# Sliding-window attention and a gated feed-forward on eight cores: earlier slots, a bias that comes by transfer, and mixing on two engines

## The reference

```python
q, k, v = x @ Wq + bq, x @ Wk + bk, x @ Wv + bv
scores = einsum('bgrsd,bgswd->bgrsw', qg, k_win)      # no scale
out = einsum('bgrsw,bgswd->bgrsd', softmax(scores), v_win)
x = layernorm(x + out @ Wo + bo)                      # called y below
x_prev = x shifted down by one row, zeros first
xr = mu_r * x + (1 - mu_r) * x_prev
xk = mu_k * x + (1 - mu_k) * x_prev
x = layernorm(x + sigmoid(xr @ W_r.T) * (square(relu(xk @ W_k.T)) @ W_v.T))
```

## Time and profile before

| | us |
|---|---|
| median of three runs | 510.74 |
| lowest to highest | 509.81 to 555.48 |
| the profiled execution | 509.77 |
| its span on the slowest core (5) | 508.2 |
| spans of all cores | 504.9 to 508.2 |

### The profile page before, as it was taken

How to read it: one execution, slowest core, us unless ns; L and a number is a source line. 1 busy time by engine, 2 the same in 40 slices (tenths; PEclk the granted TensorE clock), 3 DMA queues, 4 the chain that set the end, 5 groups by cost and what they waited for, 6 DMA issues and landing times.

```text
span 508.2 us, 10503 instructions; the slowest of 8 cores (504.9 to 508.2 us)
## 1 busy us (share of the span) xinstructions
PE 440.9 (87%) x3052; PEld 220.6 (43%) x3052; DVE 316.5 (62%) x793; ACT 333.3 (66%) x847; POOL 109.0 (21%) x298
## 2 busy tenths in 40 slices
PE   0779999999899869798898988998979988999990
PEld 0344444444444345444363353353435345464640
DVE  0056765654655587576967877877776896545421
ACT  1267868686768575776679496669658769446542
POOL 4330124130403030101122230121123032130303
PEclk9996999999999878899999999999989999999996
DMA  8999429939263646100265286567254548303112
GB/s 108 164 164 195 62 44 115 161 64 140 28 110 54 113 73 117 40 5 1 66 139 135 52 100 156 110 84 187 53 115 115 135 53 177 90 1 103 43 42 83
DMA packets 71448, 48.25 MB, mean 95 GB/s; under 512 B 59104, under 2 KB 60256, under 8 KB 71392
## 3 DMA queue, kind: packets, MB, share of 16 engines
q0 software_dynamic: 11632, 24.88, 28.1%
q1 hardware_dynamic: 59760, 22.70, 22.7%
HBM read 40.85 MB, written 8.39 MB: 97 GB/s over the span
## 4 chain that ended last, share of the span: by engine, by line
PE 59%; ACT 15%; DVE 9%; issue 8%; DMA 5%; POOL 1%; ACTq 0%; SPq 0%; DVEq 0%; POOLq 0%
PE pm L289 11%; PE pm L276 8%; PE pm L319 8%; PE pm L309 6%; PE pm L301 6%; PE po L344 6%; ACT p L383 5%; PE psc L231 4%; DVE nmax L529 4%; PE pm L255 3%; DMA bufq<-wq 2%; PE pm L291 2%; ACT junk L464 2%; DMA yT<-qy 2%; PE pm L270 1%
## 5 line engine op out<-in xcount | busy, mean ns | idle before, releaser
L383 ACT ACTIVATE p<-psc,nmax 128x320 bf16<-128x320 f32 x264 | 138.8, 540 | 96.1 <-DVE nmax L529 95.9
L529 DVE TENSOR_REDUCE nmax<-psc 128x2 f32<-128x640 f32 x132 | 108.1, 821 | 88.8 <-PE psc L237 88.2
L289 PE MATMUL pm<-w16o,ao 128*128 128x512 bf16 x272 | 66.3, 388 | 2.5 <-ACT ao L441 1.2
L541 DVE TENSOR_SCALAR p<-p,rall 128x320 bf16<-128x320 bf16 x264 | 62.4, 299 | 7.6 <-DVE rall L534 0.7
L276 PE MATMUL pm<-bufx,bufq 128*128 128x512 bf16 (+2 forms) x320 | 65.1, 350 | 1.7 <-DMA bufq<-wq 1.7
L301 PE MATMUL pm<-bufx,w16kf 128*128 128x256 bf16 x512 | 62.4, 278 | 2.1 <-ACT pt L397 1.5
L309 PE MATMUL pm<-w16r,bufx 128*128 128x512 bf16 x256 | 59.6, 379 | 5.0 <-DVE zx L565 2.2
L319 PE MATMUL pm<-w16vf,bufq 128*128 128x512 bf16 x256 | 59.5, 380 | 1.8 <-ACT pt L397 1.8
L383 ACT ACTIVATION_READ_ACCUMULATOR p<-psc,nmax 128x1 f32 x264 | 57.1, 216 | 0.0
L301 PEld LDWEIGHTS pm<-bufx,w16kf 128*128 128x128 bf16 x512 | 48.7, 99 | 14.1 <-issue 8.0
L231 PE MATMUL psc<-k,qy 64*128 64x320 bf16 x264 | 41.7, 313 | 13.5 <-ACT p L383 13.1
(11 more groups left out here) (80 smaller groups left out, 572.4 us busy)
## 6 DMA issues: line engine op xcount, KB each, us to landing
zx<-xres POOLq DMA_DIRECT2D x17, 512.0 KB, 6.3
out<-zb SPq DMA_DIRECT2D x16, 512.0 KB, 3.2
bufx<-xt POOLq DMA_DIRECT2D x16, 256.0 KB, 8.9
bufq<-wq POOLq DMA_DIRECT2D x4, 512.0 KB, 10.0
w16o<-wo POOLq DMA_DIRECT2D x8, 256.0 KB, 11.8
w16kf<-wkf POOLq DMA_DIRECT2D x8, 256.0 KB, 5.8
w16r<-wr POOLq DMA_DIRECT2D x8, 256.0 KB, 6.1
w16vf<-wvf POOLq DMA_DIRECT2D x8, 256.0 KB, 6.5
```

Source lines behind the costliest of these rows:

```text
L289: e.matmul(pm[:, bank, :], ao[:, a % 2, kc, :], w16o[:, kc, 512 * b:512 * b + 512], start=(kc == 0), stop=False)
L383: a = e.activation(p16[:, b % 2, j // 2, g, j % 2, :], psc[:, 2 * (n % 2) + g, 0:320], AF.Exp, bias=nmax[:, n % 4, g:g + 1], accum_out=sal ...
L529: e.tensor_reduce(nmax[:, n % 4, :], psc[:, 2 * (n % 2):2 * (n % 2) + 2, 0:320], mybir.AxisListType.X, ALU.max, negate=True).then_inc(s_mx, 1)
L541: t = e.tensor_scalar(part, part, rall[:, b % 2, r:r + 1], None, ALU.mult)
```

## The change

All in one edit:

- `F0` is 54 instead of 62 and `FP` 14 instead of 13: feed-forward begins eight slots earlier, and each round has two slots without a unit, not one. `NSLOT` stays 172.
- Groups 1 to 4 begin four slots earlier. As slot 4 has a unit already, a group's units are appended to a slot's list.
- The transfers of weights and x move four slots ahead with them.
- The bias matmul is gone. The bias comes as 128 equal rows; SP copies them into `zx` when y of two tiles before has been read out, and GpSimd, six slots after y, adds the residual rows with an accumulating transfer (`add_xres`). `ones` and `bo16` go.
- y is transposed as soon as it is there: `plan_y` puts each tile into the slot after `YOUT`, or after the slot in which the column copy of the round before stands, whichever is later.
- VectorE makes xk alone (`mix_k`).
- GpSimd makes xr, in two steps through an fp32 tile `part` (`mix_r`), four slots later than xk.
- k units wait for xk (`s_xk`), the first r unit of a round for xr (`s_xr`).
- A transpose into `yT` waits until GpSimd has read what was there (`s_xr`).

```diff
-F0 = 62
-FP = 13
+F0 = 54
+FP = 14
-GSLOT = (None, 8, 24, 36, 48)
+GSLOT = (None, 4, 20, 32, 44)
...
+def plan_y():
+
+    slots = {}
+    for tau in range(NT):
+        h = max(tau - 1, 0) // 2
+        free = F0 + FP * (h - 1) - 9 if h >= 1 else 0
+        slots.setdefault(max(YOUT[tau] + 1, free), []).append(tau)
+    return slots
...
                 for kc in range(KC):
-                    e.matmul(pm[:, bank, :], ao[:, a % 2, kc, :], w16o[:, kc, 512 * b:512 * b + 512],
-                             start=(kc == 0), stop=False)
-                mm = e.matmul(pm[:, bank, :], ones[:, :], bo16[:, 512 * b:512 * b + 512],
-                              start=False, stop=True)
+                    mm = e.matmul(pm[:, bank, :], ao[:, a % 2, kc, :], w16o[:, kc, 512 * b:512 * b + 512],
+                                  start=(kc == 0), stop=(kc == KC - 1))
             elif kind == "k":
                 if b == 0:
-                    e.wait_ge(s_mix, 8 * a + 8)
+                    e.wait_ge(s_xk, 8 * a + 8)
...
             elif kind == "r":
+                if a % 2 == 0 and b == 0:
+                    e.wait_ge(s_xr, 8 * (a // 2) + 8)
...
-        def mix(h, c):
+        def mix_k(h, c):
...
             e.scalar_tensor_tensor(xk[par][:, c, :], xr[par][:, c, :], muk_s[:, c:c + 1],
-                                   yT[:, par, c, 15:271], ALU.mult, ALU.add)
-            e.scalar_tensor_tensor(xr[par][:, c, :], xr[par][:, c, :], mur_s[:, c:c + 1],
-                                   yT[:, par, c, 15:271], ALU.mult, ALU.add).then_inc(s_mix, 1)
+                                   yT[:, par, c, 15:271], ALU.mult, ALU.add).then_inc(s_xk, 1)
...
+        def add_xres(tau):
+            e.wait_ge(d_bo[tau % 2], 16 * (tau // 2 + 1))
+            e.dma_start(zx[:, tau % 2, :], xres.ap()[128 * tau:128 * tau + 128, :],
+                        accum_op=ALU.add).then_inc(d_xres[tau % 2], 16)
...
+        def mix_r(h, c):
+            par = h % 2
+            e.wait_ge(s_xk, 8 * h + c + 1)
+            if 8 * h + c >= 1:
+                e.wait_ge(s_xr, 8 * h + c)
+            small(e.tensor_scalar(part[:, :], xr[par][:, c, :], mur_s[:, c:c + 1], None, ALU.mult))
+            e.tensor_tensor(xr[par][:, c, :], part[:, :], yT[:, par, c, 15:271], ALU.add).then_inc(s_xr, 1)
...
-            if n - 1 in YOUT[:NT - 2]:
-                tau = YOUT.index(n - 1)
-                e.wait_ge(s_y, tau + 1)
-                e.dma_start(zx[:, tau % 2, :], xres.ap()[128 * (tau + 2):128 * (tau + 3), :]) \
-                    .then_inc(d_xres[tau % 2], 16)
-            piece = 3 * ((n - 12) // 4) + (n - 12) % 4 if n >= 12 and (n - 12) % 4 < 3 else -1
+            if n - 6 in YOUT[:NT - 2]:
+                add_xres(YOUT.index(n - 6) + 2)
+            piece = 3 * (n // 4 - 2) + n % 4 if n >= 8 and n % 4 < 3 else -1
...
+            h, c = divmod(n - F0 + 6, FP)
+            if 0 <= h < NH and c < 8:
+                mix_r(h, c)
...
-            h, f = divmod(n - F0 + 14, FP)
-            if 0 <= h < NH and f in (0, 2):
+            for tau in YT.get(n, ()):
...
+                if half == 0 and h >= 2:
+                    e.wait_ge(s_xr, 8 * h - 8)
+                y_transpose(tau, par, 128 * half, 2 * (h // 2) + par + half)
+            if n - 1 in YOUT[:NT - 2]:
+                tau = YOUT.index(n - 1)
+                e.wait_ge(s_y, tau + 1)
+                e.dma_start(zx[:, tau % 2, :], bo_in.ap()).then_inc(d_bo[tau % 2], 16)
```

More of the change, by code:

```diff
@@ L620, in vector @@
                     shift_diff(h)
-                mix(h, c)
+                mix_k(h, c)
             for u in SLOT[n]:
@@ L731, in sync @@
         e.dma_start(cols[:, :], cols_in.ap()).then_inc(d_cols, 16)
+        e.wait_ge(d_xt[1], 64)
+        for j in range(2):
+            e.dma_start(zx[:, j, :], bo_in.ap()).then_inc(d_bo[j], 16)
         def p_transpose(b, pair):
```

32 lines of the change are left out of this document (16 added, 16 removed).

## The result

Four runs of the changed kernel have a median of 523.7 us (521.54 to 524.37), the kernel before 510.27 us beside them. The ratio is 1.026, 95% interval 1.022 to 1.031. The forecast was 497.0, with 485 to 511 as its range. A few executions of several kernels were up to a tenth longer (555.48 us once for the kernel before), most of them with the cores of a die at a lower granted clock; the ratios leave these out and the medians do not, which moves no median here by more than 0.8 us.

A forecast was written before the change was run, and what follows sets the result against it. PE (TensorE) was taken to set the pace nearly everywhere. From 509.8 us, -10 - 5 - 1 - 4 + 2 + 2 + 1 + 2 = -13 gave 497 us; forecast range 489 to 505 (0.55), outer range 485 to 511.

The forecast's parts named there:

- Parts 1 and 7: Bias matmuls leave the chain before o units, -10 us (-7 to -11); bias by transfer instead, +1 (0 to +4).
- part 7: Bias by plain then accumulating transfer into residual tiles; tiles 2 and 16 are short of time: +1 us (0 to +4).
- Part 2: Feed-forward eight slots earlier, two empty slots of 14: work moves into slots 54 to 73, -5 us (0 to -11).
- so 10.8 us leave the late stretches: Six feed-forward units of 1.8 us on PE go, three from slots 74 to 131, three from the tail.
- I take half: Third stretch (slots 54 to 73, 9.3 us PE idle): idle time can be filled only in part, so -5 us.
- Part 5: Slot 128, round 6: VectorE waits up to 6.6 us for tile 14's transposed y; +2 us (0 to +4).
- Part 4: VectorE loses 64 of 128 mix steps (30.6 us), mostly beside PE's work: -4 us (0 to -10).
- Part 6: GpSimd mixes xr in pairs of 1.3 us: nothing during attention, r(14) waits in the tail, +2 us (0 to +6).
- Part 8: GpSimd's longer steps might hold up VectorE at the shared SBUF ports: +2 us, from 0 to the first rival's price.
- The first rival: VectorE becomes the bound because GpSimd's pairs hold it up about their length: 515 to 525 us, chance 0.13.

The follow-up runs named there:

- the fourth group of experiments: Changed kernel with VectorE mixing xr (509.5 us), one change each: empty slots apart 508.2, mixing later 517.3, feed-forward from 62 499.0, from 56 502.6, from 60 499.2 us.

## Why the prediction was wrong

The measured parts, beside the kernel before: new slots +7.5, bias by transfers -8.7, GpSimd's mixing +14.2, sum +13. My sum had -4, -9 and 0.

**Parts 1 and 7 together came out right, by luck**: -9 in the sum, -8.7 under the new slots and -8.5 alone. Two terms missed in opposite directions. In part 7 I named tile 2 as the short place and gave it +1 us (0 to +4), with the transfer's median of 6.3 us. It took 13.77 us, a wait of 7.1, near the upper end of the landing times in the earlier trace rows, 15.1. That end belonged to the transfer of tile 3, issued beside the transpose of y of tile 1, and the change puts tile 2's transfer into that place. Taking the wait away is worth 6 us (502.2 to 496.1). Without it the kernel with the bias by transfers is 15 us under the kernel before (511.4 to 496.1), more than the 10.9 us of the matmuls; where the rest comes from was not looked into.

**Part 2 failed** in the step "so 10.8 us leave the late stretches". With the new slots alone slots 74 to 131 and the tail, which have six units less, are together 3 us longer. In slots 74 to 131 PE is idle for 18.2 us instead of 15.6, and the granted clock is 0.94 instead of 0.99. Empty slots under attention are a part of it: there PE waits for the chain of score, maximum and exponential, and its clock falls behind the idle time (0.72 from 276 to 288 us, in the fourth group of experiments). What else a start at 54 makes was not settled. "Below zero" was left out of the bounds. The other half, "I take half" for the third stretch, came near in number, some 5 us absorbed, but not in the idle time that it was taken from: that stayed at 9.7 us, and the granted clock rose from 0.90 to 1.00.

**Part 5 had the right wait and the wrong price.** At round 6's copy VectorE idles 5.99 us in the changed kernel and 8.84 with the new slots alone, where the part said up to 6.6; with the feed-forward from 60 a wait of 4.33 us there costs nothing. With a start at 54 it is some part of a loss of 7 us, where my term had +4 at most. The part's last sentence, that other rounds have three slots or more, does not hold for round 7: VectorE asks in slot 142 for tile 16, which is transposed in slot 143, and idles there 10.81 us before and 18.45 now.

**Part 4 was not nothing.** With pairs of the same size on GpSimd, 530.6 us with VectorE's 64 steps stand against 523.7 without them, so the relief is worth some 7 us there, inside my 0 to -10. No run relieves VectorE without loading GpSimd, and with 48 pairs in six rounds the pairs cost 2 us more than the relief gave.

**Part 6 failed, and it is the main one.** Two steps of it did. "I take VectorE's 0.48 us ... a pair of 1.3 us": the steps took 1.04 and 0.73 us, the pair 1.9, inside the bounds of 0.7 to 2.7. Worse was the count that starts "Squares end ... tile 12's at 0.1 and its norm at 2.6; two pairs follow". The order was right (five pairs, norm, two pairs, norm, one pair), but I had the five done when the squares end, and asked only when r(14) can start. In the run they begin at 472.4, because y came late, and the norm begins at 484.25, 5.9 us behind its squares. The price is not r's wait: ScalarE asks for that norm in its own order and evicts k and r behind it. Round 6 did the same some 30 us earlier, and that made the last y late: with VectorE mixing, round 7's column copy stands at 463.0, here at 470.1. I bounded the tail at +6 from the pair's length alone; PE's four idle times behind ScalarE made 11.8 us, and the two rounds in the tail cost 12. The run with pairs that nobody waits for shows that r's wait is not needed for the loss; that it goes through the queue is read from the traces, where ScalarE waits 25.2 and 23.5 us for the norms with pairs and 1.5 without.

**Part 8 had the direction right, and its price was not measured alone.** The normalisation went from 299 to 330 ns and the k mix from 479 to 514, so GpSimd's steps do hold up VectorE: 8.4 and 2.0 us of busy time. The Trainium skill, "SBUF — State Buffer", section "Who interferes with whom", says that whichever of the two comes first keeps the shared ports for the whole instruction. The trace agrees with that now for the other direction too, VectorE held up by GpSimd (330 ns against 299). In time there is only the sum of queue and port: 48 of 64 pairs cost 2 us net of VectorE's relief.

The rule of the Trainium skill, "GPSIMD Engine Reference", section "Engine selection", that GpSimd is about half as fast on two inputs, gave an estimate of 1.0 us for the addition. The trace has 0.73, 1.5 times VectorE's whole mix step. By the prediction's own count that pair of 1.8 us makes r(14) wait 3.3 us, not below 3, and the sum is 498 all the same: the pair's length alone did not decide.

Taken together, beside the kernel before: my parts 4, 6 and 8 had -4, +2 and +2 where the runs have some -7 for the relief and +21 for the pairs.

The first rival's 515 to 525 us holds the measured time, but not its mechanism: it wanted VectorE to end slower than before, and VectorE was busy 15.7 us less.

## What to carry to other kernels

Before work is given to an engine that is idle, read what else stands in its in-order queue and who waits for that, above all where a chain of small dependent steps runs through it: the price is what is queued behind, not the busy share. A stretch's mean idle time is not its room: in the third stretch here it stayed at 9 to 10 us, and the part of the new work that was absorbed came with a higher granted clock. And work taken out of a stretch shortens it only if PE does not come to wait for another engine's chain in its place. A transfer with a deadline is sized by the landing times of what stood at the place to which it moves, not by the median of all.

## What the runs showed of the hardware

- GpSimd's step with one tensor (128x256, bf16 in, fp32 out, times a column) took longer than the one with two: 1.04 against 0.73 us in the changed kernel, 1.05 against 0.75 on constants.
- With a y transpose and a bias copy beside it the DMA engines were full at 57 to 63 GB/s, and an accumulating transfer of 512 KB took 18.07 us, where the 17 of that kind had a median of 5.7 us in the changed kernel. A plain one beside a y transpose took 15.1 us in the kernel before, where the median was 6.3.
- GpSimd's steps lengthen VectorE's normalisation of 128x320 bf16 by 31 ns on average (299 to 330 in the changed kernel, 333 and 336 in two runs more), though it reads one tensor and a column.
